# Batch-wide score stacks in three buffers, one merge transfer for the quads, and a new order of the sync queue, in a gated cross-attention block with an FP4 feed-forward

## The chip, the cores and the metric

The kernel runs on one core of one Trainium2 chip. The metric is device time in microseconds of one execution. One launch does the whole block for 16 batches.

## The reference

For each of 16 batches, x is 128 x 512 (channels by positions), and so is a context c. The block is two residual steps, each scaled by the tanh of a gate:

```python
x = x + tanh(g_xattn) * xattn(layernorm(x), ctx)
x = x + tanh(g_ffn) * ffn(layernorm(x))

def xattn(x, c):                       # 8 heads of 16 channels, 512 positions
    q, k, v = Wq x + bq, Wk c + bk, Wv c + bv
    q, k = rope(q), rope(k)            # on the first 8 channels of each head
    p = softmax(q k^T / sqrt(16))
    return Wo (p v) + bo

def ffn(x):                            # FP4 weights with scales, 512 -> 1408 -> 512
    h = silu(x Wg) * (x Wu)
    y = h Wd
    return y / sqrt(mean(y * y) + 1e-6)
```

The change is in the attention part alone.

## The kernel before

All of attention is one loop over batches, each engine with a hand-written order, kept together by semaphores. A batch b has sixteen slots (`SLOTS`). In slot s TensorE (`tensor_step`, L458) makes the scores of batch b+1 for one head pair and one tile of 128 queries (`score`, L412: two matmuls of 48 rows), the transposed scores of batch b (`weigh`, L424: two matmuls of 50 rows) and a half of a value product (`values`, L435). Between them stand, each in one slot, the output projection of batch b-2 (`mix`, slot 1), the two projections of q and k for batch b+3 (`project_rot` in slot 2 and `project_pass` in slot 5; `AHEAD_PROJ` is 3) and V of batch b+1 (`project_v`, slot 8, between score and weigh). VectorE reduces the scores to row maxima (`maxima`, L666), and ScalarE takes the exponentials of the transposed scores (`exponential`, L529).

**Why there is an image in DRAM.** The scores are to be accurate to float32 with the faster float32r matmuls, so q and k are split into a rounded head and a rest. For the products head*head, head*rest, rest*head they have to lie in other rows than the projections leave them. So VectorE copies the heads (`head_rot`, `head_pass`), GpSimd subtracts (`rest_rot`, `rest_pass`), SyncE (SP) stores both into `image[n]` in DRAM (`store_head`: three transfers each, 512 KB; `store_rest`: one, 256 KB; both for the rotated and the passed channels: 1.5 MB a batch), and loads them back as `q_stack` and `k_stack` in the layout of the matmul: partitions 0 to 47 for even heads, 64 to 111 for odd ones. There are two buffers of each stack. `load_half` (L237) loads half a batch, the four heads of one "quad": four transfers of 48 rows x 4 KB, 768 KB. Between a head and its rest, the rotation needs its partners: `swap_partners` (L216) moves half rows by four transfers.

**The maxima.** Softmax needs the negative maximum of each query as two more rows of `q_stack` (rows 48 and 49, 112 and 113). VectorE turns a quad's maxima into lines (`turn_max`, L673), quad 0 in slot 7, quad 1 in slot 0 of the next step; SP stores them in DRAM (`store_max`, L250), waits, and loads them into the stack (`load_max`, L254). `weigh` waits for them at slot 0 (quad 0) and slot 8 (quad 1).

**The sums.** The value product has 16 columns of V and 16 of ones for each head, so that its rows are outputs and sums. ScalarE copies it out for each quad (`values_out`), in slot 11 and in slot 3 of the next step. SP gathers the sums (`gather_sums`), merges quad 1's rows into quad 0's tile (`merge_quads`, four transfers of 16 rows), VectorE inverts the sums in slot 6 (`invert_sums`), SP stores the inverse and loads it broadcast (`store_inverse`, `load_inverse`), and GpSimd scales the heads (`scale_heads`, L622) for `mix`.

All transfers are issued by SP alone, in the order of `sync_step` (L292) and of the prologue in front of it (L328 to L368). The transfers of one batch are 38. SP stops at a wait, and everything behind it waits too. The prologue also makes the first three batches' projections, loads the packed weights of the feed-forward part (`packed`, 1 MB), and makes all scores of batch 0 before the loop; SP stores an image there as passed and rotated parts become ready. PSUM has two banks for scores (`s_bank`), three for transposed ones (`st_bank`); a matmul into a bank waits until its reader is done.

GpSimd's order is `pool_step` (L783), VectorE's is `vector_step` (L710), ScalarE's is `scalar_step` (L552). The feed-forward part, which begins when attention has ended, is `feed_forward` (L816) and isn't touched.

## Time and profile before

| what | us |
|---|---|
| median of 3 runs | 921.22 (918.21 to 933.62) |
| the profiled execution | 918.37 |
| its span, first to last instruction | 916.6 |
| its mean granted TensorE clock | 0.945 |
| first exponential of batch 0 | 61.33 |
| last exponential of batch 15 ends | 482.6 |
| feed-forward part begins | 499.5 |

The profile is of one execution, and its times count from the span's first instruction. PE is TensorE, PEld its weight loads, DVE VectorE, ACT ScalarE, POOL GpSimd, SPq SyncE's queue of transfers. In a row of a timeline stand the start, the duration, the engine and line, the operation, the tiles (out<-in) and, in brackets, how long the engine had been idle and what ended that. For a transfer the duration is that of its issue; when it has landed shows in what waited for it.

### The profile page before, as it was taken

What the parts mean: (1) busy time and instruction counts of PE and PEld (TensorE: products, weight loads), DVE (VectorE), ACT (ScalarE), POOL (GpSimd) and SP (SyncE); (2) the same over time, 40 slices, a digit from 0 to 9 for tenths busy, and PEclk for the clock granted to TensorE, in tenths of its full rate; (3) what the DMA queues carried; (4) which work ended last, traced back from release to release, by engine and by line L of the source; (5) the groups of instructions that cost most, each with busy time, mean ns of one, the idle gap of its engine ahead of it and who ended that gap; (6) DMA issues with size and microseconds to landing.
All of it is one profiled execution on the core that took longest, in us unless ns stands there. A gap on an engine that the chain in (4) does not pass through costs nothing. (4 is left out here: it accounts for less than half of the span.)

```text
span 916.6 us, 13653 instructions
## 1 busy us (share of the span) xinstructions
PE 815.8 (89%) x5110; PEld 421.6 (46%) x5142; DVE 522.1 (57%) x760; ACT 483.6 (53%) x895; POOL 178.5 (19%) x174
## 2 busy tenths in 40 slices
PE   3378999999998988999993599999999999999997
PEld 1123333333333333334332376666666666666664
DVE  4398977888987867888871961314131423141113
ACT  2227776887787766778792552325231623252223
POOL 1232333333333423331112820000000000000000
PEclk8559999999999988999996889999999999999999
DMA  5678555666665666465212010002000110000001
GB/s 167 171 198 218 155 142 153 189 200 194 170 165 152 175 175 189 119 167 153 69 33 79 8 46 1 1 1 67 25 1 1 47 45 0 0 27 21 0 1 46
DMA packets 55176, 86.44 MB, mean 94 GB/s; under 512 B 19274, under 2 KB 20938, under 8 KB 55114
## 3 DMA queue, kind: packets, MB, share of 16 engines
q1 hardware_dynamic: 55114, 85.62, 33.0%
q8 instruction: 38, 0.62, 0.3%
q14 instruction: 24, 0.20, 0.1%
HBM read 44.70 MB, written 34.34 MB: 86 GB/s over the span
## 5 line engine op out<-in xcount | busy, mean ns | idle before, releaser
L670 DVE TENSOR_REDUCE neg_max<-s_ps 128x2 f32<-128x1024 f32 x256 | 310.0, 1219 | 61.8 <-PE s_ps L420 60.8
L536 ACT ACTIVATE probs<-st_ps 128x512 f32<-128x512 f32 x512 | 277.9, 597 | 105.5 <-PE st_ps L432 101.2
L448 PE MATMUL pv_ps<-probs,v_ones 128*32 128x256 f32 x2048 | 166.1, 397 | 12.6 <-ACT pv_sb L542 12.6
L1098 PE MATMUL gu_ps<-x_head,gu_head 128*128 128x512 f32 x352 | 155.9, 443 | 0.0
L965 DVE TENSOR_TENSOR hidden<-gu_ps,silu 128x512 f32<-128x512 f32 x44 | 30.4, 691 | 202.6 <-ACT silu L1040 202.6
L420 PE MATMUL s_ps<-k_stack,q_stack 48*128 48x512 f32 x512 | 135.4, 526 | 10.5 <-DVE neg_max L670 8.4
L1099 PE MATMUL gu_ps<-x_rest,gu_head 128*128 128x512 f32 x352 | 139.0, 395 | 0.0
L1040 ACT ACTIVATE silu<-gu_ps 128x512 f32<-128x512 f32 x44 | 26.3, 597 | 204.8 <-PE gu_ps L1101 204.8
L432 PE MATMUL st_ps<-q_stack,k_stack 50*128 50x512 f32 x512 | 110.6, 421 | 12.9 <-DMA q_stack<-max_scratch 12.7
L420 PEld LDWEIGHTS s_ps<-k_stack,q_stack 48*128 48x128 f32 x512 | 50.4, 193 | 121.1 <-issue 81.1
L1115 PE MATMUL y_ps<-dn_head,h_head 128*128 128x512 f32 x176 | 101.5, 577 | 1.1 <-DVE h_rest L967 1.0
L448 PEld LDWEIGHTS pv_ps<-probs,v_ones 128*32 128x32 f32 x2048 | 41.6, 108 | 115.2 <-ACT probs L536 94.0
L1101 PE MATMUL gu_ps<-x_bf,gu_rest 128*128 128x512 bf16 x333 | 87.4, 381 | 1.2
L1098 PEld LDWEIGHTS gu_ps<-x_head,gu_head 128*128 128x128 f32 x352 | 66.8, 190 | 17.7
L432 PEld LDWEIGHTS st_ps<-q_stack,k_stack 50*128 50x128 f32 x512 | 61.6, 191 | 24.8 <-DMA q_stack<-max_scratch 16.5
L1099 PEld LDWEIGHTS gu_ps<-x_rest,gu_head 128*128 128x128 f32 x352 | 66.3, 188 | 14.3
L1115 PE MATMUL y_ps<-dn_head,h_rest 128*128 128x512 f32 x176 | 68.4, 389 | 0.0
L1115 PE MATMUL y_ps<-dn_rest,h_bf 128*128 128x512 bf16 x163 | 63.5, 390 | 0.0
L967 DVE TENSOR_TENSOR h_rest<-hidden,h_head 128x512 fp32r<-128x512 f32 x44 | 30.5, 692 | 30.8 <-ACT h_head L1046 30.8
L1101 PEld LDWEIGHTS gu_ps<-x_bf,gu_rest 128*128 128x128 bf16 x352 | 27.4, 98 | 44.7 <-issue 24.1
L1046 ACT ACTIVATE h_head<-hidden 128x512 fp32r<-128x512 f32 x44 | 27.8, 632 | 35.3 <-DVE hidden L965 35.3
L1115 PEld LDWEIGHTS y_ps<-dn_rest,h_bf 128*128 128x128 bf16 x176 | 16.9, 96 | 47.0 <-issue 47.0
(114 smaller groups left out, 807.1 us busy)
## 6 DMA issues: line engine op xcount, KB each, us to landing
q_stack<-image SPq DMA_DIRECT2D x64, 192.0 KB, 3.9
k_stack<-image SPq DMA_DIRECT2D x64, 192.0 KB, 4.5
image<-split_head SPq DMA_DIRECT2D x32, 256.0 KB
image<-split_head SPq DMA_DIRECT2D x64, 128.0 KB
image<-split_rest SPq DMA_DIRECT2D x32, 256.0 KB
ct<-ctx_dram SPq DMA_DIRECT2D x16, 256.0 KB, 5.5
swap<-proj SPq DMA_DIRECT2D x64, 64.0 KB, 2.0
scale_of<-inverse_scratch SPq DMA_DIRECT2D x16, 256.0 KB
```

Source lines behind the costliest of these rows:

```text
L420: last = nc.tensor.matmul(out[:, odd, :], q_stack[p][rows, j, qt * P:(qt + 1) * P], k_stack[p][rows, j, :], start=True, stop=True)
L432: nc.tensor.matmul(out[:], k_stack[p][rows, j, kt * P:(kt + 1) * P], q_stack[p][rows, j, :], start=True, stop=True).then_inc(st_full, 1)
L448: last = nc.tensor.matmul(pv_ps[2 * KC * j:2 * KC * (j + 1), cols], v_ones[b % 2][:, kt, j, quad, :], probs[at % PROBS][:, j, cols], start ...
L536: nc.scalar.activation(probs[at % PROBS][:, tile % 4, :], st_ps[item % ST_BANKS][:], ACT.Exp).then_inc(st_read, 1)
L670: nc.vector.tensor_reduce(neg_max[j // 2][:, :, j % 2, qt], s_ps[item % S_BANKS][:], AXIS_X, ALU.max, negate=True).then_inc(s_read, 1)
L965: nc.vector.tensor_tensor(hidden[t % 2][:], gu_ps[t % 2][:, 1], silu[t % 2][:], ALU.mult).then_inc(hid_ok, 1)
L967: nc.vector.tensor_tensor(h_rest[t % 2][:], hidden[t % 2][:], h_head[t % 2][:].bitcast(F32), ALU.subtract).then_inc(h_rests, 1)
L1046: nc.scalar.activation(h_head[t % 2][:], hidden[t % 2][:], ACT.Copy).then_inc(h_heads, 1)
L1098: nc.tensor.matmul(gu_ps[t % 2][:, half], head, x_head[:, k], start=(k == 0), stop=False)
L1099: nc.tensor.matmul(gu_ps[t % 2][:, half], head, x_rest[:, k], start=False, stop=False)
L1101: last = nc.tensor.matmul(gu_ps[t % 2][:, half], keep["gu_rest"][:, k, col:col + P], x_bf16[:, k], start=False, stop=(k == KT - 1))
L1115: last = nc.tensor.matmul(y_ps[:, j, :], h[t % 2][:, cols], keep[w][:, t, :], start=(t == 0 and n == 0), stop=(t == IT - 1 and n == 2))
```

## The change

It does these things:

- There are three buffers of `q_stack` and `k_stack` (`STACKS`), and `load_stacks` loads a whole batch with four transfers of 48 rows x 8 KB, where `load_half` loaded halves with eight. It waits for all stores of that image and for the last `weigh` of three batches before. In `sync_step` it stands first, for batch b+2. `score` waits for it once a batch.
- The split into heads and rests is done once for rotated and passed channels together: one copy of 1024 columns in slot 11 (`split_heads`), one subtraction of 1024 on GpSimd (`split_rests`). The rotation's last step writes into `proj[:, 0]`. `store_heads` issues its six transfers at one place and `store_rests` its two, both at the end of the step. `bias_rot` waits for the rests of the batch before in place of the swap and the cosine product.
- V's columns and the ones alternate, with an offset of one column between the quads, so that quad 0's outputs lie in even rows and quad 1's in odd ones. `merge_quads` is one transfer of every second row (64). `store_inverse` is one transfer in place of two, `load_inverse` two in place of one.
- SP's order in a step and in the prologue is another. The transfers of one batch are 31.

```diff
-            def load_half(sp, n, h):
-                p = n % 2
-                for w in two:
-                    sp.wait_ge(stored[w], PARTS * (n + 1))
-                if n >= 2:
-                    sp.wait_ge(st_full, last_weight(n - 2, h))
+            def load_stacks(sp, n):
+                sp.wait_ge(stored, PARTS * (n + 1))
+                if n >= STACKS:
+                    sp.wait_ge(st_full, last_weight(n - STACKS, 1))
                 for stack, row0 in ((q_stack, 0), (k_stack, K_ROW0)):
                     for odd in two:
-                        rows = stack[p][STACK * odd:STACK * odd + DATA_ROWS, columns(h), :].bitcast(F32)
-                        heads = slice(odd * PAIRS + 2 * h, odd * PAIRS + 2 * h + 2)
-                        sp.dma_start(rows, image[n, row0:row0 + DATA_ROWS, heads, :]).then_inc(half_in[p][h], 16)
+                        rows = stack[n % STACKS][STACK * odd:STACK * odd + DATA_ROWS, :, :].bitcast(F32)
+                        sp.dma_start(rows, image[n, row0:row0 + DATA_ROWS, odd * PAIRS:(odd + 1) * PAIRS, :]).then_inc(
+                            stack_in[n % STACKS], 16)
...
             def merge_quads(sp, b):
                 sp.wait_ge(sums_in[0], 16 * (b + 1))
-                for j in range(QUAD):
-                    rows = slice(2 * KC * j + KC, 2 * KC * (j + 1))
-                    sp.dma_start(pv_sb[0][b % 2][rows, :], pv_sb[1][b % 2][rows, :]).then_inc(merged[b % 2], 16)
+                sp.dma_start(pv_sb[0][b % 2][1:P:2, :], pv_sb[1][b % 2][1:P:2, :]).then_inc(merged[b % 2], 16)
...
             def load_inverse(sp, b):
-                sp.dma_start(scale_of[:], inv_dram[b].rearrange("j h t -> (j h) t").unsqueeze(1).to_broadcast(
-                    [HEADS, KC, T])).then_inc(inverse_in, 16)
+                for h in two:
+                    sp.dma_start(scale_of[h:P:2, :], inv_dram[b, h].unsqueeze(1).to_broadcast([QUAD, KC, T])).then_inc(inverse_in, 16)
...
             def sync_step(sp, b):
                 nxt, proj_n = b + 1 < B, b + AHEAD_PROJ
-                if nxt:
-                    load_half(sp, b + 1, 1)
+                if b + 2 < B:
+                    load_stacks(sp, b + 2)
                 store_max(sp, b, 1)
+                if b:
+                    gather_sums(sp, b - 1, 1)
                 if proj_n < B:
                     swap_partners(sp, proj_n)
+                load_max(sp, b, 1)
                 if b:
-                    gather_sums(sp, b - 1, 1)
                     merge_quads(sp, b - 1)
-                load_max(sp, b, 1)
                 if b >= 2:
                     store_x(sp, b - 2)
                 if b:
                     store_inverse(sp, b - 1)
-                if proj_n < B:
-                    store_head(sp, proj_n, 1)
-                if b + 2 < B:
-                    load_half(sp, b + 2, 0)
                 if nxt:
                     store_max(sp, b + 1, 0)
+                if b + 5 < B:
+                    load_inputs(sp, b + 5)
                 if b:
                     load_inverse(sp, b - 1)
-                if proj_n < B:
-                    store_rest(sp, proj_n, 1)
-                if b + 5 < B:
-                    load_inputs(sp, b + 5)
                 if nxt:
                     load_max(sp, b + 1, 0)
+                if proj_n < B:
+                    store_heads(sp, proj_n)
                 gather_sums(sp, b, 0)
                 if proj_n < B:
-                    store_head(sp, proj_n, 0)
-                    store_rest(sp, proj_n, 0)
+                    store_rests(sp, proj_n)
...
                 swap_partners(sp, 1)
                 load_inputs(sp, 3)
-                for w in (1, 0):
-                    store_head(sp, 1, w)
-                    store_rest(sp, 1, w)
-                load_half(sp, 1, 0)
+                store_heads(sp, 1)
+                store_rests(sp, 1)
+                load_stacks(sp, 1)
                 store_max(sp, 0, 0)
                 swap_partners(sp, 2)
                 load_max(sp, 0, 0)
                 load_inputs(sp, 4)
-                for w in (1, 0):
-                    store_head(sp, 2, w)
-                    store_rest(sp, 2, w)
+                store_heads(sp, 2)
+                store_rests(sp, 2)
...
                 for slot in range(SLOTS):
                     maxima(dve, 0, slot)
                     if slot == 2:
-                        head_rot(dve, 1)
+                        split_heads(dve, 1)
                     if slot == 4:
                         statistics(dve, 3)
                     if slot == 7:
                         turn_max(dve, 0, 0)
-                    if slot == 9:
-                        head_pass(dve, 2)
-                    if slot == 14:
-                        head_rot(dve, 2)
+                    if slot == 13:
+                        split_heads(dve, 2)
...
                     if slot == 7 and b + 1 < B:
                         turn_max(dve, b + 1, 0)
-                    if slot == 7 and proj_n < B:
-                        head_pass(dve, proj_n)
-                    if slot == 11 and proj_n < B:
-                        head_rot(dve, proj_n)
+                    if slot == HEADS_AT and proj_n < B:
+                        split_heads(dve, proj_n)
```

`HEADS_AT` is 11, `PARTS` is 16 * 8. Image 0 goes the same way in the prologue: `store_heads(0)`, `store_rests(0)`, `load_stacks(0)`, where its passed part was stored before its rotated one.

## Rows read from the trace of the kernel before

**Rows 1.** The page: busy time of TensorE; its granted clock in 40 slices of the span.
```profile
PE 815.8 (89%) x5110; PEld 421.6 (46%) x5142; DVE 522.1 (57%) x760; ACT 483.6 (53%) x895; POOL 178.5 (19%) x174
...
PEclk8559999999999988999996889999999999999999
```

**Rows 2.** Windows by batch: from:to, us, busy time (xinstructions) per engine, PEclk, DMA share, GB/s.
```profile
88.77:114.57 25.80, 23.57 (x212) 9.55 (x216) 23.91 (x33) 20.03 (x38) 8.42 (x7) 1.00 0.59 167
...
332.22:362.48 30.26, 27.47 (x214) 10.45 (x218) 22.75 (x29) 20.80 (x39) 9.68 (x8) 0.89 0.58 156
...
390.55:415.85 25.30, 24.37 (x214) 9.77 (x217) 21.77 (x27) 20.40 (x38) 8.94 (x7) 1.00 0.60 165
...
439.41:462.76 23.35, 22.11 (x200) 9.44 (x200) 20.89 (x24) 18.82 (x36) 2.55 (x2) 1.00 0.23 66
```

**Rows 3.** Waits of TensorE, 60 to 500 us: in total, times, longest.
```profile
PE st_ps L432 <- DMA q_stack<-max_scratch: 12.7, 9, 1.9
```

**Rows 4.** Timeline of SP's queue, end of batch 6: start, us of issue, what.
```profile
239.34 0.86 SPq L247 DMA_DIRECT2D q_stack<-image  x2
...
241.17 0.53 SPq L252 DMA_DIRECT2D max_scratch<-max_lines  x1
...
246.46 0.56 SPq L258 DMA_DIRECT2D q_stack<-max_scratch  x2
```

**Rows 5.** Timeline of PE, the first weigh of batch 7.
```profile
249.71 0.50 PE L432 MATMUL st_ps<-q_stack,k_stack 50*128 50x512 f32 x2 [1.37 <-DMA q_stack<-max_scratch]
```

**Rows 6.** Timelines of DVE and PE in batch 12, which starts at 390.55.
```profile
402.27 0.34 DVE L687 RECIPROCAL sums<-sums 128x32 f32<-128x32 f32 x1
...
403.75 1.16 PE L408 MATMUL s_ps<-wv,ct 128*128 128x128 f32 x8 [0.19 <-DVE neg_max L670]
404.83 0.51 PE L432 MATMUL st_ps<-q_stack,k_stack 50*128 50x512 f32 x2
...
410.00 0.42 DVE L649 CAST split_head<-swap 128x512 fp32r<-128x512 f32 x1
```

**Rows 7.** Line 247's eight issues, 26 to 31 us, and their landing; the page's swap transfer.
```profile
L247 SPq DMA_DIRECT2D q_stack<-image x4: 327/393/422, 26.9 to 29.1; - x4
L247 SPq DMA_DIRECT2D k_stack<-image x4: 417/422/422, 27.7 to 30.0; - x4
...
DMA to landing us min/median/max: 3.1/4.6/6.0
...
swap<-proj SPq DMA_DIRECT2D x64, 64.0 KB, 2.0
```

**Rows 8.** Timelines of the prologue and of batch 0.
```profile
37.09 1.26 POOL L598 TENSOR_TENSOR swap<-swap,sin 128x512 f32<-128x512 f32 x1 [9.62 <-DMA swap<-proj]
...
39.36 1.22 PE L420 MATMUL s_ps<-k_stack,q_stack 48*128 48x512 f32 x3
...
43.98 0.41 DVE L649 CAST split_head<-swap 128x512 fp32r<-128x512 f32 x1
...
46.27 0.54 SPq L235 DMA_DIRECT2D image<-split_rest  x1
49.77 0.80 SPq L247 DMA_DIRECT2D q_stack<-image  x2
...
60.66 0.66 PE L432 MATMUL st_ps<-q_stack,k_stack 50*128 50x512 f32 x2
...
63.17 2.51 SPq L365 DMA_DIRECT2D packed<-gate_up_packed_dram  x2
...
68.35 1.01 SPq L247 DMA_DIRECT2D q_stack<-image  x2
...
76.23 0.50 PE L420 MATMUL s_ps<-k_stack,q_stack 48*128 48x512 f32 x2 [2.04 <-DMA k_stack<-image]
```

**Rows 9.** Timelines of SP's queue and DVE at the end of attention.
```profile
490.63 0.64 SPq L283 DMA_DIRECT2D scale_of<-inverse_scratch  x1
...
494.29 0.69 DVE L627 TENSOR_TENSOR heads_out<-pv_sb,scale_of 128x512 f32<-128x512 f32 x1 [7.64 <-DMA scale_of<-inverse_scratch]
```

More of the change, by code:

```diff
@@ L175, in attend @@
         rotated = sem("rotated")
-        pass_head = sem("pass_head")
-        pass_rest = sem("pass_rest")
-        rot_head = sem("rot_head")
-        rot_rest = sem("rot_rest")
-        stored = [sem(f"stored_{w}") for w in ("rot", "pass")]
-        half_in = [[sem(f"half_in{p}{h}") for h in two] for p in two]
+        heads = sem("heads1")
+        rests = sem("rests1")
+        stored = sem("stored1")
+        stack_in = [sem(f"stack_in{n}") for n in range(STACKS)]
         max_head = [sem(f"max_head{h}") for h in two]
@@ L185, in attend @@
         max_out = [sem(f"max_out{h}") for h in two]
-        max_in = [[sem(f"max_in{p}{h}") for h in two] for p in two]
+        max_in = [[sem(f"max_in{n}{h}") for h in two] for n in range(STACKS)]
         pv_done = sem("pv_done")
@@ L203, in attend @@
         last_weight = lambda b, quad: ST_NO["weight", b, (quad + 1) * 2 * SLOTS // QUADS - 1] + 1
+        image_rows = lambda n, first, count: keep["image"][n, first:first + count * STEP_ROWS:STEP_ROWS].rearrange("r h t -> r (h t)")
         image, max_dram, inv_dram = keep["image"], keep["max_dram"], keep["inv_dram"]
@@ L218, in swap_partners @@
                 if n:
-                    sp.wait_ge(rot_rest, n)
+                    sp.wait_ge(rests, n)
                 for at in range(0, P, 64):
@@ L573, in _ @@
                 inverse_dev(act, 0)
-                for n in range(AHEAD_PROJ):
+                for n in two:
                     bias_rot(act, n)
                     bias_pass(act, n)
-                    if n < 2:
-                        inverse_dev(act, n + 1)
+                    inverse_dev(act, n + 1)
                 act.wait_ge(scales_in, 32)
@@ L584, in _ @@
                 nc.scalar.preload_act_table_set("natural_log_exp_and_others")
+                bias_rot(act, 2)
+                bias_pass(act, 2)
                 act.wait_ge(consts, 8)
```

136 lines of the change are left out of this document (58 added, 78 removed).

## Prediction

> **What bounds the kernel now.** I read the page first: TensorE is busy for 89% of the span, and its granted clock dips inside the attention part [rows 1]. Then the span was cut into one window per batch, each beginning at that batch's first exponential, sixteen windows from 61.33 to 482.60, 421.27 us together [rows 2]. The reader is to see that batches of equal work differ: batch 12 takes 25.30 us, batch 10 takes 30.26, batch 14 (no projections any more) 23.35. TensorE's busy time in batch 12 is 24.37 of 25.30, so 25.30 is the pace without a wait for data. Next the waits [rows 3]: of what stops TensorE, 12.7 us are nine waits of the weigh (L432) for the rows of maxima, up to 1.9 long, and 2.04 one wait for k_stack in batch 0 [rows 8]. So the loop is TensorE at its own pace plus a late transfer at the start of most batches; the feed-forward part is not touched and I take it as fixed.
>
> Why that transfer is late shows in SP's queue and TensorE's timeline [rows 4, 5]. The store of the maxima (L252) is issued at 241.17, behind four stack loads issued from 239.34. SP's next load of maxima goes out only at 246.46, when that store has landed, and TensorE's first weigh of the next batch starts at 249.71 after 1.37 idle. 5.3 us pass between the issues of a 16 KB store and the load that needs it: it queued behind 768 KB.
>
> From 88.77 to 439.41, batches 1 to 13, the loop takes 350.6 us. Eleven batches at 25.30, batch 1 without mix (about 24.2) and batch 13 at about 23.4 would be 325.9. So 24.7 us are there to be won: the waits, and the stretches at half clock after some of them (batch 10 ran at 0.89 of the clock against 1.00 in batch 12 [rows 2]).
>
> **The change, steady batches.** Quad 0's maxima: the bulk loads go to the start of the step, so their store no longer queues behind them. It leaves when DVE has the maxima, some 14 us into the batch, the load some 3 us later, 7 us before the need. That wait goes.
>
> What is late next is quad 1. `load_stacks` now stands first in the step and waits for all eight stores of that image; the last are issued at the end of the step before. All four loads (1.5 MB) then stand ahead of quad 1's store of maxima. The chain, from a batch's start S, with batch 12 as the measure of the slots [rows 6]: the second split copy runs at 410.00, which is 5.85 before the next batch's start (415.85). The merged copy has twice the elements: 0.8 us (between 0.42 and 0.84), so it ends at S-5.05. Six head stores at about 0.6 of issue: S-1.5; a gather 0.6; rests (GpSimd 2 x 1.26 [rows 8], done at S-2.5, hidden): the second rest store issues at S-0.4. Issue to landing of such a store behind three others was 3.5 (46.27 to 49.77 [rows 8]). Twice the bytes are queued now, but over twice the issue time: 3.5, between 2.0 (the swap's on the page [rows 7]) and 5. The stack loads start at S+3.2 (1.6 to 4.6).
>
> 1.5 MB of stack loads, issued at once: first issue 26.9, last issue 30.0 and 6.0 to landing, so 9.1 us; the first took 3.1, the seven others 0.86 each [rows 7]. Half the DMAs of twice the size need the same if the bytes set it: 9.1 (bounds: 3.1 + 0.86 x 3 = 5.7 if each DMA costs its time whatever its size; 11.3 if other traffic slows it as in rows 4, where half the bytes and the small store took 7.1 us instead of 5.7). Quad 1's store of maxima lands with them, S+12.3. The load follows: 0.3, the second issue 0.3, landing 2.0 (the swap's [rows 7]; at most 3.0, which is 246.46 to 249.71 less 0.3): S+15.0. The weigh that needs it, slot 8, started at 404.83, S+14.28. So a stall of 0.75, near 0.8.
>
> DVE gives the same from its side. Its reciprocal of the sums ran at 402.27, S+11.7; the gather of sums is now queued behind the stack loads too and lands at S+12.4. Behind that reciprocal DVE has the reduce of slot 7 (1.2), for which TensorE's projection of V waits (403.75, already after 0.19 of waiting): the V step moves by 0.8. The two stalls are in series on TensorE and do not add: the first takes the second's place. The copy of the passed half moves out of this stretch of DVE and comes back at slot 11: nothing to 0.2, in the range.
>
> The pace becomes 26.1. Batches 1 to 12: 12 x 26.1 = 313.2. In batch 13 the projections are gone but the late load is not: 15.0 and then the rest of the batch from slot 8 (25.30 - 14.28 = 11.0): 26.0. Together 339.2 against 350.6: **-11.4**.
>
> Hidden or nothing: the merge in one transfer (64 rows, same bytes) saves 1.9 us of SP's issue; SP then waits anyway. Loads of inputs and `load_inverse` fall between S+15 and S+18, where SP has room, and head stores wait for DVE. `bias_rot` now waits for the rests, done 2 us before the batch ends. `scale_heads` ends about 2 us before its mix. V written at every second column: the same 682 ns, at most twice that (then +0.3 a batch). TensorE's value matmuls keep 32 contiguous columns.
>
> **The change, prologue and batch 0.** Here it costs. Before, one half (768 KB) and its maxima were enough to go on; now whole batches are loaded. Step by step: image 0's eight stores all stand behind the rotation now, four of them stood before it; at 0.6 each the last goes 2.4 later, so the loads start at 29.2 (26.9 before [rows 7]) and land at 38.3, and the first scores start there instead of 39.36: -1.0. `split_heads(1)` ends near 43.9 (the rotated half's copy began at 43.98 before [rows 8]). But its eight stores are now all behind it: the last is issued at 48.0, lands 3.5 later, and stack 1 loads from 51.6 (49.77 before) and lands at 60.7, the swaps of image 2 behind it at 61.7; GpSimd's two steps (2 x 1.26) give 64.3. DVE stands at `split_heads(2)` in slot 13 of batch 0's maxima, with two reduces behind it, from about 58 on at its pace of before. The copy ends at 65.1, the reduce of slot 14 at 66.3, and TensorE's first score of batch 1 waits for that bank. The first weigh starts at about 66.8 instead of 60.66: **+6.2**.
>
> Batch 0: image 2's stores and 1 MB of packed weights go before its stacks. From 65.1, eight stores take 4.6 of issue and the packed loads 5.1 (63.17 to 68.35), so SP comes to `load_stacks(2)` at 74.8. With the same 2.2 of backlog as then (76.2 - 68.35 - 5.7, where 5.7 is 3.1 + 3 x 0.86) and 9.1, they land at 86.1, quad 1's maxima at 88.8. Unstalled, slot 8 comes at 81.9 (76.23 less its 2.04 of waiting, 1.5 for the score and V before it, plus 6.2). A stall of 6.9 in place of 2.04: +4.9, and a clock that falls behind so long a wait, +2 (batch 10 is 4.96 over the pace at a clock of 0.89, of which no more than 1.9, the longest wait of rows 3, is waiting): **+6.9**.
>
> Tail: three merges fewer before the last inverse take 1.9 off the chain to DVE's last `scale_heads` at 494.29; two broadcasts in place of one put back 0.6 of issue and something of landing: near 0.
> By the Trainium skill (DMA: Bandwidth & Descriptors, "Why a DMA increments its semaphore by 16 and not by 1") the slowest dimension of both sides picks how many DMA engines share a transfer; the broadcast's source has 4 there now and had 8. By it the tail would be about +1 and the sum 1 us longer; the trace shows only the 3.7 us from issue (490.63) to use [rows 9], and no row of the new form.
>
> **The sum:** -11.4 + 6.2 + 6.9 = +1.7. The profiled execution took 918.37 (span 916.6), so 920.1 by it; the median of the runs, 921.22, stands 2.85 above it, so I forecast **923**. Within 2% is about what a measurement of this kernel can tell from no change.
>
> **Rivals.**
> A. As forecast: the wait moves from slot 0 to slot 8 and the start pays. 0.55; 905 to 935 by the bounds on the store's landing.
> B. The loads with 8 KB rows land in about 6 us. For it: the lower bound above. Against: 192 KB per 0.86 us was steady over seven loads. Then the maxima are at S+12, no stall in the loop: 12 x 25.3 + 23.6 = 327.2, -23.4; the two loads of the prologue and that of batch 0 each come 3 earlier: +6 in place of +13.1: 904 on the median's scale. 0.20, half of it beyond 2%.
> The skill speaks against B (SBUF — State Buffer, "Door 1: The DMA port swizzle"): bandwidth goes with the ports the partitions reach, and 48 partitions of one half reach 8 of 16, whatever the row length; half of its 436 GB/s is 218, an estimate, and the trace's 192 KB in 0.86 us is 228: it agrees, and by it the loads stay at 9.
> C. Slower: the eight stores bunched at the end of a step land at S+5 instead of S+3.2, with SP held at `load_stacks` meanwhile. For it: everything of an image, 1.5 MB, is now issued in 5 us. Each us there is 13 us in all; at 1.8 it is 923 + 23 = 946, and it decides against the change from a landing at S+4.6 on. Against: stores of 768 KB landed 3.5 behind the last issue. 0.17.
> D. The maxima come as forecast, but the clock falls as often as before (some 8 us more at half pace): 931. 0.08.
>
> Faster by over 2% (under 902.8): half of B and a little: 0.12. Slower by over 2% (over 939.6): C and the edge of A: 0.20. Same: 0.68. The range takes in B's centre and most of C: 904 to 942.
>
> **What would show it.** Right: no wait of L432 for maxima at a batch's first weigh, but one at slot 8, and one of the V projection (L408's line) for DVE; the reciprocal of sums waiting for its gather every batch; batch windows near 26.1 and even; the first exponential near 67.5 instead of 61.3; a wait of 5 to 8 us in batch 0; SP's longest waits at `load_stacks` for the rest stores. Wrong: windows at 25.3 (B), over 27 (C), a first weigh before 63.

## The result and the profile after

The changed kernel takes **1003.88 us** (median of 4 runs, 996.81 to 1010.19) against 919.72 (median of 4, 917.85 to 933.62; a fourth run joined the three behind the 921.22 that the forecast went by): a ratio of **1.092, 95% interval 1.081 to 1.103**. Slower by 9%, where 923 us and no measurable change were forecast, and outside the range. Its profiled execution has a span of 994.4 us against 916.6, at a mean granted clock of 0.897 against 0.945.

The page of the changed kernel, the lines that answer to [rows 1] and the stack transfers of its last part (count, KB each, us from issue to landing; before: 192.0 KB, 3.9 and 4.5):
```profile
PE 847.4 (85%) x5142; PEld 432.9 (44%) x5142; DVE 525.7 (53%) x743; ACT 483.9 (49%) x895; POOL 176.8 (18%) x160
...
PEclk9557699989588986989989877999999999999999
...
q_stack<-image SPq DMA_DIRECT2D x32, 384.0 KB, 6.2
k_stack<-image SPq DMA_DIRECT2D x32, 384.0 KB, 9.4
```
The same matmuls (some records are missing from the page of before, 5110 against 5142; the weight loads are equal) and 32 us more of busy TensorE: that is clock, not work. It dips through the whole attention part where before it dipped a few times.

The windows by batch of the changed kernel, columns as in [rows 2], batches 0, 1, 5, 6, 7, 9, 10 and the sum:
```profile
73.90:114.00 40.10, 32.30 (x188) 11.74 (x192) 22.32 (x28) 19.78 (x38) 7.57 (x6) 0.63 0.66 159
114.00:138.60 24.60, 23.66 (x212) 9.51 (x216) 22.56 (x29) 20.01 (x38) 8.18 (x6) 0.99 0.67 152
...
233.20:272.00 38.80, 32.90 (x214) 12.14 (x218) 23.19 (x29) 20.96 (x39) 9.41 (x7) 0.69 0.57 140
272.00:300.70 28.70, 27.41 (x214) 10.51 (x218) 23.20 (x29) 20.91 (x40) 9.47 (x7) 0.89 0.57 140
300.70:331.80 31.10, 26.79 (x214) 10.76 (x212) 22.94 (x29) 20.73 (x39) 9.44 (x7) 0.89 0.62 151
...
363.60:398.90 35.30, 31.52 (x214) 11.14 (x212) 23.48 (x29) 20.90 (x39) 9.43 (x7) 0.76 0.61 154
398.90:424.50 25.60, 24.47 (x215) 9.77 (x218) 22.97 (x29) 20.79 (x39) 9.47 (x7) 1.00 0.67 156
...
sum 486.40, PE 422.16 PEld 166.92 DVE 352.12 ACT 324.76 POOL 126.61; mean PE 26.38 PEld 10.43 DVE 22.01 ACT 20.30 POOL 7.91
```
The windows are anything but even: batch 10 shows that the pace is still 25.6, batch 5 takes 38.80 for the same instructions. Of the 77.7 us by which the last batch ends later (560.3 against 482.6), 12.6 lie before the first exponential (73.9 against 61.3), 12.7 in batch 0 (40.1 against 27.4), and 52.6 in batches 1 to 13 (114.00 to 517.20 is 403.2, against 350.6); batches 14 and 15 are as they were. Over those thirteen one window of each kernel splits the 52.6, before first:
```profile
88.77:439.41 350.64, 325.42 (x2724) 128.45 (x2728) 292.73 (x370) 267.18 (x500) 116.88 (x96) 0.97 0.60 166
```
```profile
114.00:517.20 403.20, 349.14 (x2724) 138.58 (x2728) 296.63 (x358) 267.70 (x501) 113.92 (x84) 0.88 0.60 143
```
23.7 us are a longer busy TensorE (clock 0.88 against 0.97), 28.8 are longer idle. The idle has a name in the waits of TensorE and VectorE, 70 to 575 us (total, times, longest):
```profile
DVE sums L660 <- DMA sums<-pv_sb: 52.5, 12, 10.6
...
PE s_ps L394 <- DVE neg_max L643: 45.6, 14, 5.7
```
The weigh's nine waits for maxima [rows 3] are gone, as forecast; V's projection (L394) now waits 3.6 to 5.7 us in ten of the thirteen batches, and no more than 0.4 in batches 1, 6 and 10. How that comes shows in batch 7, which starts at 300.70. SyncE's queue:
```profile
304.01 0.77 SPq L244 DMA_DIRECT2D q_stack<-image  x2
304.83 0.89 SPq L244 DMA_DIRECT2D k_stack<-image  x2
305.76 0.55 SPq L250 DMA_DIRECT2D max_scratch<-max_lines  x1
306.51 0.60 SPq L264 DMA_DIRECT2D sums<-pv_sb  x1
...
315.49 0.85 SPq L256 DMA_DIRECT2D q_stack<-max_scratch  x2
```
The landing of those four loads (line L244, 303 to 316 us):
```profile
L244 SPq DMA_DIRECT2D k_stack<-image x2: 422/422/423, 304.8 to 305.3; - x2
...
DMA to landing us min/median/max: 4.4/7.3/9.9
```
VectorE, then TensorE:
```profile
315.75 0.35 DVE L660 RECIPROCAL sums<-sums 128x32 f32<-128x32 f32 x1 [3.30 <-DMA sums<-pv_sb]
316.02 1.16 DVE L643 TENSOR_REDUCE neg_max<-s_ps 128x2 f32<-128x1024 f32 x1
```
```profile
317.24 2.07 PE L394 MATMUL s_ps<-wv,ct 128*128 128x128 f32 x8 [3.58 <-DVE neg_max L643]
319.25 0.79 PE L418 MATMUL st_ps<-q_stack,k_stack 50*128 50x512 f32 x2
```
The loads are issued at S+3.3 (forecast S+3.2) and the last lands at 315.2, 11.2 us later (forecast 9.1). The 8 KB of sums issued behind them arrive with them; VectorE stands at the reciprocal, the reduce behind it frees the bank that V needs, and TensorE idles 3.58. Then it runs at half clock: V takes 2.07 us instead of the 1.16 of [rows 6].

The three batches without the stall show the other half of it. In batch 10 the loads leave 0.15 us behind the batch's start and not 3.3, and V waits only 0.40 although they take 11.7 us:
```profile
399.05 0.78 SPq L244 DMA_DIRECT2D q_stack<-image  x2
```
```profile
412.34 1.16 PE L394 MATMUL s_ps<-wv,ct 128*128 128x128 f32 x8 [0.40 <-DVE neg_max L643]
```
Batches 1, 6 and 10 are the ones that follow batches 0, 5 and 9, the slowest (clock 0.63, 0.69 and 0.76). At half clock the end of a batch is longer, so its stores are issued earlier before the next batch begins (the last at S-3.4 in batch 10, at S-0.2 in batch 7), and the loads leave at S-0.9 to S+0.2.

The start, SyncE's queue of the prologue and of batch 0, and TensorE's two waits there:
```profile
50.62 1.18 SPq L235 DMA_DIRECT2D image<-split_rest  x2
55.85 0.81 SPq L244 DMA_DIRECT2D q_stack<-image  x2
```
```profile
72.65 0.80 PE L406 MATMUL s_ps<-k_stack,q_stack 48*128 48x512 f32 x2 [10.97 <-DVE neg_max L643]
73.22 0.66 PE L418 MATMUL st_ps<-q_stack,k_stack 50*128 50x512 f32 x2
...
95.88 0.80 PE L418 MATMUL st_ps<-q_stack,k_stack 50*128 50x512 f32 x2 [7.72 <-DMA q_stack<-max_scratch]
```

### The profile page after: what moved, and what is told of

Same layout as the page of the kernel before. It is cut to its first block and busy times, and to the rows that moved or that the text cites. A ratio compares the mean times of both kernels' runs of the same rounds, so it can differ in the third digit from the quotient of the medians.

```text
span 994.4 us, 13465 instructions
## 1 busy us (share of the span) xinstructions
PE 847.4 (85%) x5142; PEld 432.9 (44%) x5142; DVE 525.7 (53%) x743; ACT 483.9 (49%) x895; POOL 176.8 (18%) x160
## 5 line engine op out<-in xcount | busy, mean ns | idle before, releaser
L434 PE MATMUL pv_ps<-probs,v_ones 128*32 128x256 f32 x2048 | 180.4, 428 | 10.5 <-ACT pv_sb L525 10.5
L406 PE MATMUL s_ps<-k_stack,q_stack 48*128 48x512 f32 x512 | 142.6, 553 | 31.3 <-DVE neg_max L643 18.8
L418 PE MATMUL st_ps<-q_stack,k_stack 50*128 50x512 f32 x512 | 118.3, 450 | 7.7 <-DMA q_stack<-max_scratch 7.7
L406 PEld LDWEIGHTS s_ps<-k_stack,q_stack 48*128 48x128 f32 x512 | 52.7, 203 | 154.2 <-issue 86.4
L1065 PE MATMUL gu_ps<-x_bf,gu_rest 128*128 128x512 bf16 x352 | 91.2, 382 | 0.0
L1062 PEld LDWEIGHTS gu_ps<-x_head,gu_head 128*128 128x128 f32 x352 | 66.8, 190 | 17.8
L418 PEld LDWEIGHTS st_ps<-q_stack,k_stack 50*128 50x128 f32 x512 | 64.4, 208 | 17.9 <-DMA q_stack<-max_scratch 7.9
L394 PE MATMUL s_ps<-wv,ct 128*128 128x128 f32 x128 | 27.6, 383 | 51.4 <-DVE neg_max L643 45.6
L1079 PE MATMUL y_ps<-dn_rest,h_bf 128*128 128x512 bf16 x176 | 68.6, 390 | 0.0
L591 POOL TENSOR_TENSOR split_rest<-proj,split_head 128x1024 fp32r<-128x1024 f32 x15 | 35.6, 2371 | 82.4 <-DVE split_head L628 82.4
L394 PEld LDWEIGHTS s_ps<-wv,ct 128*128 128x128 f32 x128 | 23.4, 274 | 57.7 <-DVE neg_max L643 50.4
```

The costliest lines, as they stand in the source:

```text
L394: last = nc.tensor.matmul(out[:, 0, k * P:(k + 1) * P], ct[n % C_TILES][:, k * P:(k + 1) * P], wv[:], start=True, stop=True)
L406: last = nc.tensor.matmul(out[:, odd, :], q_stack[p][rows, j, qt * P:(qt + 1) * P], k_stack[p][rows, j, :], start=True, stop=True)
L418: nc.tensor.matmul(out[:], k_stack[p][rows, j, kt * P:(kt + 1) * P], q_stack[p][rows, j, :], start=True, stop=True).then_inc(st_full, 1)
L434: last = nc.tensor.matmul(pv_ps[2 * KC * j:2 * KC * (j + 1), cols], v_ones[b % 2][:, kt, j, 2 * KC * quad:2 * KC * (quad + 1)], probs[at % ...
L591: ops.tensor_tensor(split_rest[:], proj[:], split_head[:].bitcast(F32), ALU.subtract).then_inc(rests, 1)
L1062: nc.tensor.matmul(gu_ps[t % 2][:, half], head, x_head[:, k], start=(k == 0), stop=False)
```

## The experiments

The theory on seeing this: the place of `load_stacks` ahead of small transfers is the loss, and each wait costs about as much again in clock (the runs below bear out the first, not the fixed rate of the second). Rivals: the transfers' form (8 KB rows; broadcasts from four source rows), the merge, the start. Ratios are to the kernel before in the same series, whose median lay between 919.72 and 930.01, so times of different series compare to about 1%; "loop" is batches 1 to 13, first exponential to first exponential, in the profiled execution.

**One remedy at a time, on the changed kernel.** First the row length:
```diff
-    sp.dma_start(rows, image[n, row0:row0 + DATA_ROWS, odd * PAIRS:(odd + 1) * PAIRS, :])
+    for h in two:
+        rows = stack[n % STACKS][STACK * odd:STACK * odd + DATA_ROWS, columns(h), :].bitcast(F32)
+        sp.dma_start(rows, image[n, row0:row0 + DATA_ROWS, odd * PAIRS + 2 * h:odd * PAIRS + 2 * h + 2, :])
```


> The changed kernel with each stack transfer of 48 rows x 8 KB cut into two of 48 rows x 4 KB (eight a batch), at the same place of the queue. Theory Q (the loads stand ahead of the gather of sums and of quad 1's maxima, and 8 KB rows make them slower: 11.7 us from first issue to last landing instead of 9.1): they land in about 9.3 again, the wait of the V projection shrinks from 3 to 5 us to about 1 to 2, the clock falls less often, and the time comes to 940 to 965. Rival R (the row length doesn't matter, bytes or the stores before them set the landing): last landing stays near 11.5 and the time within 1% of 1004.

Measured 993.49, ratio 1.075 (1.071 to 1.079). V's waits fall from 45.6 to 27.5 us, and the busy stretches at half clock stay. Row length is a part, not the cause. The time is far outside the theory's 940 to 965 and near the other answer's. The loads did not come back to 9.3 us: over the kernel's sixteen they took 10.1 to 12.0 us from first issue to last landing, where the changed kernel's took 10.8 to 13.0. And the loop stayed as long as it was: 401.5 us against 403.2, since TensorE's busy time grew by what the waits lost, from 349.1 to 366.4 at a clock of 0.84.

`load_stacks(b + 2)` moved behind quad 1's `load_max`:
```diff
-                if b + 2 < B:
-                    load_stacks(sp, b + 2)
                 store_max(sp, b, 1)
...
                 load_max(sp, b, 1)
+                if b + 2 < B:
+                    load_stacks(sp, b + 2)
```


> The changed kernel with load_stacks moved from the head of the step to behind load_max of quad 1, nothing else. Theory Q: the gather of sums and quad 1's maxima are no longer queued behind 1.5 MB, the V projection's wait for VectorE is gone, periods of batches 1 to 13 come from 31 to 25.3 to 26.5, the time to 925 to 945 (prologue and batch 0 keep some 15 to 20 us of their loss); quad 0's maxima may be late again by up to 1 us. Rival R (the merged split, the bunched stores or the strided V are what stalls): the periods stay over 29 and the time over 980.

Measured 981.92, 1.061 (1.057 to 1.065). V's wait is gone and another stands in its place, at the first weigh of each batch:
```profile
PE st_ps L418 <- DMA q_stack<-max_scratch: 39.9, 14, 4.0
```
SyncE now stands at `load_inverse` for the inverse's store, which was issued behind the bulk, and the next batch's maxima stand behind that. Its longest wait, its queue at 246 us, and TensorE:
```profile
SPq L279 <- DMA inverse_scratch<-sums: 88.5, 13, 8.3
```
```profile
246.78 1.17 SPq L279 DMA_DIRECT2D scale_of<-inverse_scratch  x2
248.00 0.76 SPq L256 DMA_DIRECT2D q_stack<-max_scratch  x2
```
```profile
253.05 0.80 PE L418 MATMUL st_ps<-q_stack,k_stack 50*128 50x512 f32 x2 [3.32 <-DMA q_stack<-max_scratch]
```
So the theory's 925 to 945 is missed, and the number is nearer the rival's (over 980, periods over 29); but what TensorE waits for is not what the rival named, it is the next transfer in the queue. The loop took 401.0 us, against 403.2 in the changed kernel: nearly all that was won lies in batch 0, which took 25.8 instead of 40.1.

The reciprocal moved on VectorE behind what V waits for:
```diff
-                    if slot == 6 and b:
+                    if slot == 8 and b:
```

> The changed kernel with VectorE's reciprocal of the sums moved from slot 6 to behind V's take-over in slot 8. Theory Q1 (the wait of V for VectorE goes, but quad 1's maxima land at about 17 us of a batch where they are needed at 14.3): the wait moves to the weigh of slot 8 and shrinks by about 1 us a batch, time 975 to 995. Rival Q2 (only the sums are late): the waits vanish, time about 930 to 945.

Measured 998.69, 1.078 (1.073 to 1.084). V's wait goes, the weigh of slot 8 takes it over: ten waits, 34.9 us, up to 5.9, a little over the theory's 975 to 995. That is the "in series" of the prediction, the same transfers seen by another instruction.

The start alone: the packed weights' loads ahead of step 13, the prologue's `split_heads(dve, 2)` from slot 13 to the last slot.
```diff
+                for b in range(B - 3):
+                    sync_step(sp, b)
...
-                for b in range(B):
+                for b in range(B - 3, B):
...
-                    if slot == 13:
+                    if slot == SLOTS - 1:
                         split_heads(dve, 2)
```


> The changed kernel with batch 0 and the prologue alone touched: the loads of the first two packed weights of the feed-forward part moved from batch 0 to ahead of step 13, and the prologue's third split_heads block placed behind the last of the transposes that it stood between. Theory (batch 0's 12.7 us over before are the wait for stack 2's bulk behind those 3 MB and the 11.3 us of the prologue's block waiting for VectorE): first exponential at 70 instead of 73.9, batch 0 at 33 to 36 instead of 40.1, the loop's later batches as in the changed kernel, time 990 to 996. Rival (those waits only uncover the next one): first exponential and batch 0 within 1.5 us of the changed kernel's, time 1000 to 1006.

Measured 1005.24, 1.084 (1.076 to 1.092). The first exponential came at 70.6, as the theory said, batch 0 took 42.9, where it did not: the packed loads were in nobody's way, since `load_stacks(2)` left at 81.51 without them (81.53 with them), held by its own image's stores. The theory falls for batch 0. (The packed loads are 1 MB, not the 3 MB of the expectation.)

**Parts of the change, on the kernel before.** The one-transfer merge with interleaved quads, the inverse in one store and two broadcasts, nothing else:
```diff
-                for j in range(QUAD):
-                    rows = slice(2 * KC * j + KC, 2 * KC * (j + 1))
-                    sp.dma_start(pv_sb[0][b % 2][rows, :], pv_sb[1][b % 2][rows, :])
+                sp.dma_start(pv_sb[0][b % 2][1:P:2, :], pv_sb[1][b % 2][1:P:2, :])
...
-                sp.dma_start(scale_of[:], inv_dram[b].rearrange("j h t -> (j h) t").unsqueeze(1).to_broadcast(
-                    [HEADS, KC, T])).then_inc(inverse_in, 16)
+                for h in two:
+                    sp.dma_start(scale_of[h:P:2, :], inv_dram[b, h].unsqueeze(1).to_broadcast([QUAD, KC, T]))
```


> The kernel before with V's columns and the ones alternating, one merge transfer in place of four, one store of the inverse and two broadcasts: this part of the change alone. SP's issue in a step gets 1.9 us shorter, and in the kernel before SP reached quad 0's store of maxima some 3 us after they were ready. If that is what made them late (theory Q), the store leaves up to 1.9 us earlier, most of the waits of the first weigh go with the clock falls behind them, and the time falls by 10 to 20 us, to 900 to 910. Rival (SP's order, not its load, made them late; or the strided V costs VectorE): within 0.5% of before.

951.91, 1.030 (1.026 to 1.034): neither answer, since the theory had it faster and the rival within 0.5%. Then the same with the inverse stored twice, so that each broadcast reads eight source rows:
```diff
-                sp.dma_start(inv_dram[b].rearrange("h j (x e) -> (h j x) e", e=32), sums[:])
+                for copy in two:
+                    for h in two:
+                        sp.dma_start(inv_dram[b, h, :, copy], sums[64 * h:64 * h + 64, :])
```

> b_merge with the inverse stored twice in DRAM (four small stores), so that each broadcast reads eight source rows and not four. Theory K (four source rows confine the 256 KB broadcast to four DMA engines, and quad 0's load of maxima queues behind it there): the load lands 1 to 1.5 us earlier after its issue than in b_merge, the waits of the first weigh fall from 2 to 3 us towards 1 to 1.5, the clock falls less often, time 925 to 940. Rival (the broadcast's form does not matter; other order effects made b_merge slow): 950 or more, since there are three more transfers to issue.

926.03, 1.002 (0.998 to 1.007). The waits of the first weigh in the two, without and with the second copy:
```profile
PE st_ps L430 <- DMA q_stack<-max_scratch: 24.4, 13, 3.0
```
```profile
PE st_ps L432 <- DMA q_stack<-max_scratch: 12.2, 10, 1.8
```
So where the maxima stand behind the broadcast, the time hangs on its source rows, 2.8% between the two.
The Trainium skill (DMA: Bandwidth & Descriptors, "Why a DMA increments its semaphore by 16 and not by 1") says that a transfer with few rows in its slowest dimension is shared by few DMA engines. The shorter waits with eight source rows agree with that; how many engines took part, no trace here shows.

The other way: keep the transfers, move the maxima in front.
```diff
+                if nxt:
+                    store_max(sp, b + 1, 0)
                 if proj_n < B:
                     store_head(sp, proj_n, 1)
+                if nxt:
+                    load_max(sp, b + 1, 0)
                 if b + 2 < B:
                     load_half(sp, b + 2, 0)
-                if nxt:
-                    store_max(sp, b + 1, 0)
...
-                if nxt:
-                    load_max(sp, b + 1, 0)
```


> The kernel before with SP's order alone changed: quad 0's store of maxima goes ahead of the passed head stores, and its load ahead of the half-batch load, the broadcast, the rest store and the inputs. Theory M (SP's order behind slot 7 makes quad 0's maxima late, and each wait near 2 us also costs a fall of TensorE's clock): no wait of the first weigh is left, batches 2 to 12 take 25.3 to 25.6, the time falls by 20 to 25 us, to about 897 to 903 where before is 921. Rival N (the half-batch load, now some 2 us later, becomes what TensorE waits for, or another bound near 27): the time stays within 1%.

909.86, 0.984 (0.975 to 0.993): between the two answers; the waits of the first weigh are gone (0.3 us are left). With the merge on top:

> b_merge and the order of b_max_first together. If the alternating columns and the merge cost nothing themselves (theory M), the time is that of b_max_first within 0.5%, near 900. If the strided V or the merge costs VectorE or TensorE something of its own, it stays 1% or more above b_max_first.

912.56, 0.985 (0.977 to 0.992): with the maxima ahead, the broadcasts cost nothing that can be told. In both, what is late next is the mix, which waits for the scaled heads, here in the run with the merge:
```profile
PE st_ps L454 <- POOL heads_out L625: 10.2, 10, 1.5
```

**The remedies together.** On the changed kernel: 4 KB rows, loads late, and the next maxima ahead of the inverse:
```diff
-                if b:
-                    load_inverse(sp, b - 1)
                 if nxt:
                     load_max(sp, b + 1, 0)
+                if b:
+                    load_inverse(sp, b - 1)
```

> The changed kernel with three edits together: 4 KB rows, load_stacks behind quad 1's load of maxima, and quad 0's load of maxima ahead of the broadcast. Theory Q with M: nothing bulky or confined stands ahead of a small load that TensorE needs, so batches 1 to 13 take 25.3 to 26 and the clock stays up; what is left is the prologue and batch 0: 930 to 945. Rival: something else of the change (merged split, bunched stores) holds the period over 28: over 970.

967.07, 1.047 (1.039 to 1.055). All waits for maxima are gone, and the mix at slot 1 takes over in full: 37.5 us in 12 waits of up to 3.8, since the inverse's broadcasts now stand behind the maxima. The theory's 930 to 945 is missed again, by a wait that was hidden before.

So the mix moves by two slots, first on the kernel before with the maxima ahead:
```diff
-MIX_AT, ROT_AT, PASS_AT, V_AT = 1, 2, 5, 8
+MIX_AT, ROT_AT, PASS_AT, V_AT = 3, 2, 5, 8
```

> The kernel before with the maxima of the next batch issued ahead of SyncE's bulk transfers, as in b_max_first (909.9 us, 0.984), and the mix of each batch moved from slot 1 to slot 3 of the next one. Theory (the 6.3 us of waits of the mix on heads_out, and the clock falls behind them, are what keeps the period over 25.3): those waits go, the periods of batches 1 to 13 come to 25.3 to 25.8, and the time to 893 to 902. Rival (the period is set by something else that the waits only mark): the waits go and the time stays at 905 to 912.

**891.86, 0.964 (0.958 to 0.970)**, a little under the theory's range. Its batches 1 to 13 as one window:
```profile
90.60:413.70 323.10, 313.03 (x2724) 126.66 (x2724) 295.80 (x370) 267.14 (x500) 116.24 (x96) 1.00 0.62 180
```
Clock 1.00 in the mean, periods of 25.0, no wait for data over 0.6 us. No version was clearly faster. With the packed loads out of batch 0 as well (the first two edits of a_prologue),

> The kernel before with the maxima first, the mix at slot 3, and the two packed weights' loads out of batch 0. Theory: periods as in b_max_first_mix3 and batch 0 at 25.5 instead of 27.4, so 1 to 3 us under b_max_first_mix3: 890 to 900. Rival: the packed weights arriving beside step 13 delay the maxima there, and it is even with or slower than b_max_first_mix3.

it is 895.38, 0.966 (0.960 to 0.972): no gain. Batch 0 took 28.1, not 25.5, and the batch that got those loads 33.6.

With merge and mix at 3:

> The kernel before with the one-transfer merge, the interleaved quads and the two broadcasts from four rows, and with the maxima first and the mix at slot 3. Theory (the broadcast hurt only because the next maxima stood behind it): within 6 us of b_max_first_mix3, 888 to 898. Rival (four-row broadcasts cost by themselves): 905 or more.

893.27, 0.959 (0.953 to 0.965), even with the one without the merge. And the changed kernel with everything (4 KB rows, loads late, maxima first, inverse twice, mix at 3):

> The changed kernel with each remedy that helped alone: stack transfers cut to rows of 4 KB, load_stacks behind quad 1's maxima, the next batch's first maxima ahead of the inverse broadcasts, the inverse stored twice so that a broadcast reads eight source rows, and the mix at slot 3. Theory (four late transfers, each with a clock fall behind it, are the whole loss of the loop): no wait over 1.5 us in batches 1 to 13, periods of 25.3 to 26.2, granted clock of the run 0.94 or more; what is left over the kernel before is the prologue and batch 0, some +12 to +20 us, less the 7 that the kernel before itself loses by its own waits: 925 to 945. Rival (the merged, bunched stores and loads hold the queue whatever the order): periods of 27.5 or more remain, with a time over 955.

914.78, 0.988 (0.981 to 0.995), better than the theory's best. The three buffers and the bunched stores are in it, so these are not the loss of the loop.

**Leaving one remedy out of a_all** tells what each is worth where no other wait hides it. Each edit is the reverse of one above: `load_stacks` first, `MIX_AT` at 1, rows of 8 KB, one copy of the inverse.

> a_all with load_stacks put back to the head of SyncE's step, as in the changed kernel; everything else of a_all stays. Theory (the place of the bulk ahead of quad 1's maxima and of the gather of the sums is the main loss): waits of V's projection for VectorE and of the weigh at slot 8 come back, some 2 us a batch with the clock falling behind them, +35 to +55 us over a_all, 950 to 970. Rival (row length or the broadcasts are the main loss and the place only exposes them): under +15, 915 to 930.

999.12, 1.076 (1.069 to 1.083): **84 us over a_all**, more than the theory's 35 to 55. In the profiled executions the loop is 76 us longer (410.8 against 334.9) and batch 0 14.5 (40.5 against 26.0).

> a_all with the mix back at slot 1. Theory (inverse broadcasts behind the maxima land too late for slot 1, a wait of 1 to 2 us in most batches and a clock fall behind some): +12 to +30 us over a_all, 927 to 945. Rival (eight-row broadcasts land in time): within 5 us of a_all.

958.74, 1.031 (1.023 to 1.039): 44 over, above the theory's 12 to 30.

> a_all with the stack transfers back at rows of 8 KB, four a batch. Theory (a bulk that stands behind the maxima has 14 us of room, so 11.7 us instead of 10.1 for it matter little): within 6 us of a_all, 912 to 922. Rival (8 KB rows block the DMA engines for the broadcasts and the next maxima too): over 925.

924.22, 0.996 (0.992 to 1.000): 9 over, between the two answers. The runs of the two kernels do not overlap, but they are from two series, and by the ratios the intervals just do.

> a_all with one copy of the inverse in DRAM, so that each broadcast reads four source rows as in the changed kernel. Theory (the mix at slot 3 has room for it, but the transfers behind it on the same DMA engines have not): +10 to +28 us over a_all, 925 to 943. Rival (with the maxima ahead of it the broadcast disturbs nothing): within 5 us of a_all.

907.82, 0.978 (0.971 to 0.984): 7 *under* a_all; neither answer. The second copy makes four stores of one, 2.3 us of issue for 0.5, ahead of the next maxima's; that these cost the 7 us is likely, and not shown. Fewer source rows hurt nobody any more.

The loops of a_all, of it with the loads first, and with the mix at slot 1:
```profile
98.80:433.70 334.90, 317.20 (x2724) 126.72 (x2723) 298.04 (x358) 267.12 (x501) 113.07 (x83) 0.99 0.73 177
```
```profile
113.80:524.60 410.80, 376.23 (x2724) 142.67 (x2727) 297.65 (x358) 268.91 (x500) 113.67 (x84) 0.82 0.58 141
```
```profile
101.10:480.90 379.80, 333.62 (x2724) 130.03 (x2724) 293.47 (x358) 267.92 (x501) 113.42 (x83) 0.94 0.65 155
```
In the second, the waits for V came back (31.2 us, nine of them between 1.5 and 4.5), and the busy time alone grew by 59 us.

Last, the order alone, with every transfer of the changed kernel as it is: `load_stacks` late, the next maxima ahead of the inverse, mix at 3.

> The changed kernel with its transfers untouched; only three places in the order: load_stacks behind quad 1's maxima, the next maxima ahead of the inverse broadcasts, the mix at slot 3. Theory (what costs is the order, the transfers' form is worth some 9 us for the row length): 914 to 922, a ratio of 0.985 to 0.995. Rival (8 KB rows and four-row broadcasts together collide): over 930.

**919.22, 0.986 (0.979 to 0.993)**: three places in the order are worth 1.092 against 0.986. The fair comparison for the rest of the change is the kernel before with its own order mended, b_max_first_mix3, at 0.964. The loop of a_order_only, and TensorE's largest wait for GpSimd in it:
```profile
102.10:440.20 338.10, 319.38 (x2725) 127.48 (x2728) 293.84 (x354) 267.64 (x500) 113.12 (x83) 0.98 0.73 174
```
```profile
PE st_ps L442 <- POOL heads_out L605: 3.8, 6, 1.1
```

## Why the prediction was wrong

**Right in mechanism.** Quad 0's wait vanished; the new one stood where the prediction put it, at V's projection waiting for VectorE, behind the reciprocal waiting for its gather. The stack loads left at S+3.3 (S+3.2). The stores landed as forecast in the loop (the loads left at S+3.3 to S+3.8 in nine of the ten stalled batches, at S+5.1 in batch 5 alone), so rival C's mechanism did not happen but for that batch, although its mark, windows over 27, did. The pace without a wait was 25.6 (batch 10). The tail and the feed-forward part did not move.

**The step that failed: "the first took 3.1, the seven others 0.86 each ... 9.1".** In the ten stalled batches it was 11.2 to 13.0, 11.8 in the mean, so even the upper bound, 11.3, was too low. "A stall of 0.75, near 0.8" became 3.6 to 5.7, 4.5 in the mean. In batch 7, the mildest but one, 2.1 us are the loads, 0.4 the gather behind them (315.2 to 315.75 less the 0.1 allowed), 0.1 their start. I had set 11.3 as the bound and 9.1 as the value, though [rows 4] already showed 7.1 for what an idle queue does in 5.7. The forecast stall was the small difference of two long times, so an error of 2 to 4 us in 9.1 multiplied it. Over the thirteen batches V waited 45.4 us, where some 12 were forecast (12 of 0.8, and 2.6 in batch 13). The forecast also took every batch alike; the record shows that a stall with a long stretch at half clock behind it spares the next batch its own.

**The term that was missing: the clock behind a stall.** "The pace becomes 26.1" has no clock in it, while for batch 0 the same text allowed 2 us behind a long wait. TensorE's busy time in the loop was 349.1 us against some 314 at full clock: 35 us. The two, 33 and 35, are the 64 between the forecast loop (339.2) and the measured 403.2, to within 4. This is the account of this one run; the second term does not follow from the first by a fixed rate. In a_rows4k V waited 27 us in the loop and not 45, and TensorE was busy for 366.4. Rival D gave this 8 us by "as often as before". Before, waits were at most 1.9 us and cost about their own length again: 12.7 us of waits, and 12.4 of busy time (325.4 against the 313.0 of b_max_first_mix3). In the changed kernel it was 36 us of busy time for 45.4 of waits.

**The start, +6.2 forecast, +12.6 measured.** Each step is late by what loads and stores take longer: stack 0 lands at 41.8 (38.3), `split_heads(1)` ends at 46.7 (43.9), the rest stores end at 51.8 and the loads leave at 55.85, 4.65 behind the last store's issue (3.5; 51.6), land near 67.0 (60.7), the swaps behind them at 67.9, first weigh 73.22 (66.8). Here too the size of the bulk was the error, 11.7 and 11.2 for 9.1, and the rest store's landing 1.1. **Batch 0, +6.9 forecast, +12.7 measured:** the wait is 7.72 against 6.9, so the step was sized well (it allowed 11.3 us for the loads with their backlog, and they took 12.4); the clock behind it (0.63 in that window) cost 5 us more than the 2 allowed.

**Broadcast from four rows: "tail would be about +1".** The rule was weighed in the tail alone. In every batch the broadcast stood ahead of the next maxima; b_merge against b_merge_dup shows 2.8% for it. In the changed kernel it was covered by the larger wait. In a_loads_late the load of maxima issued at 248.00 behind the broadcasts was used 5.05 us later, against 3.25 before (246.46 to 249.71); how much of that is the source rows was not separated there.

**The order of causes**, as the repaired kernel sizes them. Bulk first: 84 us. Rows of 8 KB: some 9. The 44 us of the mix at slot 1 are not among the changed kernel's losses, where the mix never waited in the loop: they are what the re-ordered inverse would have cost. Merge: nothing that could be told. Bunched stores and three buffers: at most the 4.7 us of loop below, beside the start; neither was taken out by itself. The start keeps the changed design behind: a_all_one_copy has its first exponential at 73.3 and a loop of 327.8, b_max_first_mix3 62.2 and 323.1; batch 0 takes 28.4 in both, and 11.1 + 4.7 are the 16 us between their medians. What in the start could be won back was not found: the one try there failed.

## What to carry to other kernels

A transfer queue is a place in line: in these runs a bulk load issued first made the small transfers behind it as late as itself, so issue what is needed soonest and is small first, and give the bulk the buffer's slack. Where a forecast margin is under a microsecond and the transfer it rests on takes nine, take the size seen under traffic, and price the stall with the clock behind it, as a range: in these loops the clock cost from 0.7 to 2 times what the waits took. When several late transfers stand in a row, removing one shows the next (1.092 to 1.061, 1.075, 1.078 one at a time, 0.988 together); leaving one out of the repaired kernel sizes them.

## What the runs showed of the hardware

**Row length.** 384 KB in 48 rows of 8 KB landed 2.26 us apart in the changed kernel (308.45, 310.76, 313.07, 315.24 in batch 7), 174 GB/s; cut into 192 KB with rows of 4 KB, 1.02 us apart (301.51 to 308.62 over seven), 194 GB/s, and in the prologue of the kernel before 0.86, 228 [rows 7]. Landing of a_rows4k's eight, issued from 298.2 to 301.3:
```profile
DMA to landing us min/median/max: 3.3/5.4/7.3
```
They take 10.4 us in all for 1.5 MB, against 11.2. Over all sixteen loads of each kernel it is 10.1 to 12.0 against 10.8 to 13.0. In the mean that is 10.9 against 11.7, so row length explains some 0.8 us of the gap to the 9.1 of [rows 7]. The rest stays open: the first set of a_rows4k's loads, as many bytes in rows as long as those of [rows 7] and in the same place of the prologue (the order within the eight differs), took 11.1. With the loads behind the maxima the difference was worth some 9 us of the whole (a_all_8k against a_all).
The Trainium skill (SBUF — State Buffer, "Door 1: The DMA port swizzle") counts the ports that the partitions reach, half of them for 48 partitions of one half. The 228 agrees to within 5% with the 218 that the prediction worked out from its figure, an estimate; the 194 and the 174 lie below it.

**The clock's price.** Loops of equal work: busy TensorE 313.0 us with no wait over 0.6; 325.4 with nine of up to 1.9; 333.6 with twelve of up to 2.8 (a_all_mix1); 343.2 with twelve of up to 3.0 (b_merge); 349.1 with ten of 3.6 to 5.7; 366.4 with waits of up to 5.1, 27 us in all (a_rows4k); 376.2 with nine of 1.5 to 4.5, 31 us in all (a_all_loads_first). The last three show that the price isn't the wait's length alone: V waited 45 us in the first of them and 27 and 31 in the others, and these lost more to the clock. In the changed kernel the granted clock stayed at half, 1.2 GHz, for 3 to 11 us behind eight of its ten waits and for 17 and 30 behind two; in a_all_loads_first for 13 to 31 us behind six of nine. The longest stretch there lies behind the shortest wait, 1.5 us:
```profile
284.00:314.00 30.00, 30.00 (x152) 9.38 (x153) 17.55 (x22) 15.73 (x28) 5.96 (x5) 0.50 0.59 142
```
TensorE is busy in all 30 us of that window, at a clock of 0.50. What decides between short and long was not tried. The start shows it as well: batch 0 took 26 to 43 us in these kernels, 36.6 in b_merge_order with no wait of more than 1.8 us in it, at a clock of 0.59.
